# State-space scan of a decoder kernel: TensorE adds half of the decayed state, VectorE the other half by 256 columns

## The reference, cut to what matters

```
dA = exp(dt[..., None] * A)
h  = dA * h + dt[..., None] * B[:, None, :] * x[..., None]
y  = einsum('ben,bn->be', h, C)
```

## Time and profile before

| | |
|---|---|
| median of 3 runs | 6723.25 us (6720.93 to 6724.89) |
| span of the profiled execution | 6765.1 us |
| its granted TensorE clock, mean | 0.858 of full speed |
| busy in the span: PE, DVE, ACT, POOL | 73%, 77%, 50%, 47% |
| the stage of the change | about the first 2640 us |

### The profile page before, as it was taken

One profiled execution on the slowest core, in us unless ns is written; L12 is line 12 of the kernel. 1 busy time (PEld: TensorE's weight loads), 2 busy tenths in 40 slices (PEclk: granted clock), 3 DMA queues, 4 the chain that ended last, 5 costly groups with the idle time before them and its releaser, 6 DMA issues. The chain is left out here.

```text
span 6765.1 us, 148097 instructions
## 1 busy us (share of the span) xinstructions
PE 4948.8 (73%) x49380; PEld 2831.3 (42%) x49380; DVE 5218.7 (77%) x9423; ACT 3364.1 (50%) x4743; POOL 3159.4 (47%) x2904
## 2 busy tenths in 40 slices
PE   4777777777777776587775965899966647877890
PEld 1222222222222223365555543666645545666440
DVE  3999999999999997498886334677759947888344
ACT  3555555555655554355662210444446626777440
POOL 5433333333333422366652655555533317988443
PEclk8888888888888888699897986899978868999995
DMA  1111111111111112221112552000001112222343
GB/s 41 39 39 46 40 40 42 43 39 40 46 39 39 43 40 63 59 60 41 43 37 68 143 115 84 15 17 18 14 25 32 32 36 71 73 73 75 115 138 102
DMA packets 620376, 366.38 MB, mean 54 GB/s; under 512 B 67337, under 2 KB 601292, under 8 KB 619852
## 3 DMA queue, kind: packets, MB, share of 16 engines
q1 hardware_dynamic: 600524, 335.54, 17.8%
q0 software_dynamic: 11648, 21.26, 1.5%
q10 hardware_dynamic: 7680, 3.15, 0.2%
HBM read 204.83 MB, written 66.85 MB: 40 GB/s over the span
## 5 line engine op out<-in xcount | busy, mean ns | idle before, releaser
L1363 ACT ACTIVATE mb_dA<-ps,mb_a_neg 128x1024 f32<-128x1024 f32 x1008 | 1122.5, 1114 | 768.9 <-PE ps L1133 684.7
L1707 DVE TENSOR_TENSOR mb_m<-mb_dA,ps 128x512 f32<-128x512 f32 x2016 | 1284.6, 677 | 29.3 <-PE ps L1148 17.5
L1715 DVE TENSOR_TENSOR ps<-mb_m,ps 128x512 f32<-128x512 f32 x1984 | 1272.8, 685 | 42.3 <-PE ps L1148 42.1
L1148 PE MATMUL ps<-mb_ur,mb_bl 64*128 64x256 bf16 x4032 | 452.6, 308 | 495.3 <-DVE mb_m L1707 487.8
L1160 PE MATMUL ps<-mb_m,mb_cz 128*32 128x256 f32 x8064 | 745.5, 446 | 3.7 <-DVE mb_m L1707 2.6
L1148 PEld LDWEIGHTS ps<-mb_ur,mb_bl 64*128 64x128 bf16 x4032 | 122.3, 98 | 1044.5 <-DVE mb_m L1707 982.6
L1133 PE MATMUL ps<-mb_ur,mb_sel 64*128 64x256 bf16 x4032 | 455.3, 310 | 121.9 <-ACT mb_dA L1363 96.0
L677 POOL TENSOR_TENSOR x_p<-x_p,x_rec 128x2048 f32<-128x2048 f32 x64 | 231.7, 3620 | 212.2 <-DVE x_rec L838 212.1
L1133 PEld LDWEIGHTS ps<-mb_ur,mb_sel 64*128 64x128 bf16 x4032 | 154.6, 103 | 418.1 <-ACT mb_dA L1363 265.8
L1160 PEld LDWEIGHTS ps<-mb_m,mb_cz 128*32 128x32 f32 x8064 | 169.2, 115 | 269.9 <-issue 226.7
L1614 POOL TENSOR_TENSOR mb_ys<-mb_ys,mb_cbu 128x256 f32<-128x256 f32 x64 | 46.6, 728 | 487.3 <-ACT mb_ys L1444 487.3
(11 more groups left out here) (494 smaller groups left out, 13041.2 us busy)
## 6 DMA issues: line engine op xcount, KB each, us to landing
mb_ur<-mb_pc SPq DMA_DIRECT2D x768, 64.0 KB
mb_bl<-mb_pc SPq DMA_DIRECT2D x576, 64.0 KB
ef_w<-in_ef_w SPq DMA_DIRECT2D x35, 514.5 KB
mx_w<-in_mx_w SPq DMA_DIRECT2D x39, 384.0 KB
moe_made<-mx_y SPq DMA_DIRECT2D x39, 256.0 KB
ea_wqk<-in_ea_wqk SPq DMA_DIRECT2D x70, 129.0 KB
ea_wvo<-in_ea_wvo SPq DMA_DIRECT2D x70, 128.5 KB
ea_x<-hidden SPq DMA_DIRECT2D x280, 32.0 KB, 2.0
```

Of the source, the lines that this page charges most:

```text
L1148: mm = nc.tensor.matmul(ps[:, UB + 2 * (t % 2) + g, 256 * pl:256 * pl + 256], bl[k, j % 2, tl, 128 * pl:128 * pl + 128], ur[k, j % 2, tl], ...
L1363: nc.scalar.activation(dA[:, t % RING].rearrange("p (g n) -> p g n", g=2), ps[:, DT:DT + 2, :], ACT.Exp, scale=a_neg[:, 0:1]).then_inc(dA_ ...
L1707: nc.vector.tensor_tensor(m[:, t % RING, half], dA[:, t % RING, half], ps[:, UB + 2 * ((t - 1) % 2) + g, :], ALU.mult).then_inc(m_ready.se ...
L1715: nc.vector.tensor_tensor(u, m[:, t % RING, 512 * g:512 * g + 512], u, ALU.add).then_inc(h_ready.sem, 1)
```

## The change

The bank `g = 1` of the state (`PE_PART`, columns 512 to 1023) is no longer added by DVE. DVE multiplies it by its decay (`decay_pe_part`, 512 columns), and PE adds `m` onto the outer product that already stands in the bank, as a product with the identity (`add_decayed`, `start=False`). The other bank stays with DVE, in two parts of 256 columns each (`decay_part`, `add_part`). The next `decay_pe_part` waits for the product of PE (`hp_ready`).

```diff
+        PE_PART = slice(512, 1024)
+        DVE_PARTS = [slice(0, 256), slice(256, 512)]
...
                 def outer(i, t):
...
-                                                  start=True, stop=True)
+                                                  start=g == 0 or pl == 0, stop=g == 0, skip_group_check=g == 1)
                     mm.then_inc(ub_done.sem, 1)
+
+                def add_decayed(i, t):
+                    pe.wait_ge(mp_ready.sem, mp_ready.at(i, t))
+                    nc.tensor.matmul(state(t, PE_PART), ident[:], m[:, t % RING, PE_PART], start=False, stop=True,
+                                     skip_group_check=True).then_inc(hp_ready.sem, 1)
...
                     for t in range(T):
...
+                        if 1 <= t < T - 1:
+                            add_decayed(i, t)
                         if t + 3 < T:
                             spread_dt(i, t + 3)
...
-                def decayed(i, t, g):
...
-                def advanced(i, t, g):
...
+                def decay_pe_part(i, t):
+                    dve.wait_ge(dA_ready.sem, dA_ready.at(i, t))
+                    dve.wait_ge(y_summed.sem, before(y_summed, i, t))
+                    if t == 1:
+                        dve.wait_ge(ub_done.sem, ub_done.at(i, 1))
+                    else:
+                        dve.wait_ge(hp_ready.sem, hp_ready.at(i, t - 1))
+                    nc.vector.tensor_tensor(m[:, t % RING, PE_PART], dA[:, t % RING, PE_PART], state(t - 1, PE_PART),
+                                            ALU.mult).then_inc(mp_ready.sem, 1)
...
                     for t in range(T):
                         j, tl = t // 16, t % 16
                         if t >= 1:
-                            decayed(i, t, 0)
-                            decayed(i, t, 1)
+                            decay_pe_part(i, t)
+                        if t >= 2:
+                            add_part(i, t - 1, 0)
+                            add_part(i, t - 1, 1)
...
-                        if 1 <= t < T - 1:
-                            advanced(i, t, 0)
-                            advanced(i, t, 1)
+                        if t >= 1:
+                            decay_part(i, t, 0)
+                            decay_part(i, t, 1)
```

More of the change, by code:

```diff
@@ L1007, in mamba @@
         ub_done = st.counter("ub_done", T - 1)
-        m_ready = st.counter("m_ready", 2 * (T - 1))
-        h_ready = st.counter("h_ready", 2 * (T - 2))
+        mp_ready = st.counter("mp_ready", T - 1)
+        md_ready = st.counter("md_ready", 2 * (T - 1))
+        hp_ready = st.counter("hp_ready", T - 2)
+        hd_ready = st.counter("hd_ready", 2 * (T - 2))
         y_summed = st.counter("y_summed", T - 1)
@@ L1018, in mamba, with state @@
         y_ready = st.counter("y_ready")
+        PE_PART = slice(512, 1024)
+        DVE_PARTS = [slice(0, 256), slice(256, 512)]
+        def state(t, cols):
+            g = cols.start // 512
+            return ps[:, UB + 2 * (t % 2) + g, cols.start - 512 * g:cols.stop - 512 * g]
         def xc(u, f, j):
@@ L1139, in outer @@
                     if t >= 2:
-                        pe.wait_ge(m_ready.sem, m_ready.at(i, 2 * (t - 1)))
+                        pe.wait_ge(md_ready.sem, md_ready.at(i, 2 * (t - 1)))
                     else:
-                        pe.wait_ge(m_ready.sem, m_ready.at(i - 1, 2 * (T - 1 - t)))
+                        pe.wait_ge(md_ready.sem, md_ready.at(i - 1, 2 * (T - 1 - t)))
                     if tl == 0:
@@ L1157, in contract @@
                         pe.wait_ge(y_taken.sem, y_taken.at(4 * i + j - 1))
-                    pe.wait_ge(m_ready.sem, m_ready.at(i, 2 * t))
+                    pe.wait_ge(mp_ready.sem, mp_ready.at(i, t))
+                    pe.wait_ge(md_ready.sem, md_ready.at(i, 2 * t))
                     for pr in range(4):
@@ L1361, in decay @@
                     act.wait_ge(dt_done.sem, dt_done.at(i, t))
-                    act.wait_ge(m_ready.sem, before(m_ready, i, t, 2))
+                    act.wait_ge(md_ready.sem, before(md_ready, i, t, 2))
                     nc.scalar.activation(dA[:, t % RING].rearrange("p (g n) -> p g n", g=2), ps[:, DT:DT + 2, :], ACT.Exp, scale=a_neg[:, 0:1]).then_inc(
@@ L1696, in weigh_bc @@
                     nc.vector.tensor_reduce(cb[:], cb_prod[:], AX.X, ALU.add).then_inc(cb_ready.sem, 1)
-                def decayed(i, t, g):
[L1699 to L1703, removed]
-                    if t > 1:
[L1705 to L1708, removed]
@@ L1711, in advanced, with decay_part, add_part @@
+                def decay_part(i, t, g):
+                    if t > 1:
+                        dve.wait_ge(hd_ready.sem, hd_ready.at(i, 2 * (t - 2) + g + 1))
+                    cols = DVE_PARTS[g]
+                    nc.vector.tensor_tensor(m[:, t % RING, cols], dA[:, t % RING, cols], state(t - 1, cols),
+                                            ALU.mult).then_inc(md_ready.sem, 1)
+                def add_part(i, t, g):
                     if g == 0:
                         dve.wait_ge(ub_done.sem, ub_done.at(i, t + 1))
-                    dve.wait_ge(m_ready.sem, m_ready.at(i, 2 * (t - 1) + g + 1))
@@ L1714, in advanced @@
-                    u = ps[:, UB + 2 * (t % 2) + g, :]
-                    nc.vector.tensor_tensor(u, m[:, t % RING, 512 * g:512 * g + 512], u, ALU.add).then_inc(h_ready.sem, 1)
+                    dve.wait_ge(md_ready.sem, md_ready.at(i, 2 * (t - 1) + g + 1))
+                    cols = DVE_PARTS[g]
+                    h = state(t, cols)
+                    nc.vector.tensor_tensor(h, m[:, t % RING, cols], h, ALU.add).then_inc(hd_ready.sem, 1)
                 def output(i, j):
```

## The result

The changed kernel takes **6933.1 us** (median of 4 runs, 6929.96 to 6937.52) against 6723.18 (6720.93 to 6724.89) for the kernel before on the same chip: a ratio of 1.0313, 95% interval 1.0301 to 1.0326, or +210 us. The forecast was 7035 with 6935 to 7165.

What follows compares the result with a forecast made beforehand. DVE was taken to bound the kernel before, PE after the change: 169.4 us of PE work + 4.3 stalls + 3.5 clock = 177.2 us a chunk against 157.7, +312 us over 16 chunks, giving 7035 us, range 6935 to 7165.

Steps and rivals of the forecast that it cites:

- PE's work alone is longer than the chunk of today: Main point: PE's products in a chunk, start to start at full clock, sum to 169.4 us against 157.7.
- The ring: DVE multiply, hand-over to PE, add, hand-over back: 1.91 us, under PE's 2.27 us step, so priced at nothing.
- the low clock stays: Rival, chance 0.08: PE keeps 28% of its time at the lower clock level, 7363 us.
- the slow handshake: Rival, chance 0.05: slower DVE-PE hand-overs cost 0.2 us in some 37 plain steps a chunk, 7153 us.
- The add is cheaper: Rival, chance 0.05: hidden weight loads make each of 62 adds cost 0.86 us, 6837 us.
- 62 adds x 1.06", "14 extras x 1.06", "17 small extras x 0.64: PE's work in a chunk: add_decayed 65.7 us, other products of 512 columns 14.8, small ones such as gates 10.9.
- 19.5 us: Growth forecast for each of 16 chunks, from 157.7 to 177.2 us, giving +312 us.
- Idle PE: Stalls of PE a chunk: 2.1 us behind norm and 2.2 behind silus, together 4.3 us.
- the 0.36 of slack: Plain step: the 1.91 us from DVE's multiply through PE's add back to DVE is 0.36 under PE's 2.27.
- The clock: Lower PE clock only behind the norm and silus stalls: 3.5 us a chunk, from 0 to 6.
- faster: Rival, chance 0.04: DVE stays the bound, an add costing 0.53 us as one record, 6504 us.
- the break-even: Price of each of 62 adds at which a chunk takes as long as before: 0.75 us.

Runs made afterwards that it cites:

- a mix by steps: Kernel before, with TensorE adding only in steps without an extra product, TensorE's products reordered, norm's two small operations on GpSimd: 6587.6 us, ratio 0.9785.
- the same order and `norm` and the add in all steps: Changed kernel with TensorE's order spread_dt, extra product, add_decayed, contract, outer, and norm's two small operations on GpSimd: 6796.7 us, ratio 1.0100.

## Why the prediction was right or wrong

**Right in kind.** "PE's work alone is longer than the chunk of today" holds: doubling a group on PE costs all of its 0.22 us a step after the change and nothing before it, the plain step is 2.27 us to the hundredth, and DVE waits in it. The ring is not the bound: PE waits for the multiply 50 us in the whole kernel. The rise of the clock to 0.98 came as forecast, so "the low clock stays" is out, and with the plain step at 2.27 so is the slow handshake. None of the four rivals happened. "The add is cheaper" was the nearest, but it gave its 0.2 us to every add, and the plain step shows that it isn't there.

**Wrong in size, +312 forecast and +210 measured.** From its first multiply to its last, the stage ran from 112.86 to 2624.8 us before and runs from 113.03 to 2837.8 now, 212.8 us longer. (The two spans differ by 170.5 only, because what stands behind the stage was 42 us longer in the profiled execution of the kernel before.) Two terms of the sum account for it.

1. *The extras' and adds' prices were start-to-start distances with another neighbour.* Rows 5 give 1.06 ahead of bf16 work, and rows 6 give 0.64 ahead of bf16 work. In the changed kernel nearly each extra stands ahead of the add, and the pair costs 0.2 us less; the prediction turned this saving down by rows 5, which have no such pair. The 33 pairs make 6.6 us; with `turn_y` (0.28 measured, 0.44 charged) PE's work in a chunk is about 162.3 us, not 169.4. The step that failed is the list "62 adds x 1.06", "14 extras x 1.06", "17 small extras x 0.64".
2. *19.5 us were charged to 16 chunks.* The last two chunks have fewer extras. By the windows shown first they take 158.58 + 146.77 = 305.4 us; the kernel before took 154.67 + 152.23 = 306.9 for them, by these windows of it:

```profile
2320.10:2474.77 154.67, 112.54 (x1082) 40.14 (x1082) 151.12 (x259) 89.71 (x102) 54.17 (x39) 0.82 0.15 40
2474.77:2627.00 152.23, 101.94 (x1044) 36.95 (x1040) 150.70 (x256) 76.08 (x83) 16.26 (x18) 0.81 0.11 29
```

The 39 us charged to them are not there. The sum holds for 14 chunks, which grew by (212.8 + 1.6) / 14 = 15.3 us each, from 157.7 to 173.0.

Against these stand the stalls, which were charged too little. With each start-to-start distance on PE set against the same distance at full clock, the first 14 chunks of the trace take 162.3 us of work, 6.8 of idle PE and 3.9 of lower clock on average, together 173.0; 169.4, 4.3 and 3.5 were forecast.

- *Idle PE, 6.8 for 4.3.* `norm` stops PE for 3.5 us a chunk, and 2.1 was forecast, because GpSimd now holds DVE for 2.26 us in one instruction instead of about 1: `norm` keeps DVE from 1393.59 to 1397.66, 4.07 us for 2.47, and less the 0.36 of slack that is 3.7. `silus` stops PE for 2.6 (2.2 forecast). The rest is 0.2 in nearly every chunk and 1.5 to 3.2 us at the boundary behind three of them.
- *The clock, 3.9 for 3.5.* This term was right. The lower level comes behind `norm` in each of the 14 chunks, by these windows of one:

```profile
1398.00:1402.00 4.00, 3.61 (x19) 1.22 (x20) 3.58 (x10) 1.61 (x3) 3.92 (x2) 0.73 0.02 4
1402.00:1406.00 4.00, 4.00 (x28) 0.90 (x30) 2.46 (x7) 1.11 (x1) 2.25 (x2) 0.84 0.00 0
```

Behind `silus` it comes in some chunks and not in others, after the same 2.54 us of idle PE. In one, `contract` ran at the lower level (1.01 us from start to start, a record of 1.08) and the add behind it took 2.01; in another, `contract` ran at full clock (a record of 0.64):

```profile
997.58 0.61 PE L1142 MATMUL ps<-mb_ur,mb_sel 64*128 64x256 bf16 x4 [2.54 <-ACT mb_dA L1380]
998.11 1.08 PE L1175 MATMUL ps<-mb_m,mb_cz 128*32 128x256 f32 x8
999.12 0.61 PE L1157 MATMUL ps<-mb_ur,mb_bl 64*128 64x256 bf16 x4
999.66 2.08 PE L1164 MATMUL ps<-mb_m,mb_ident 128*128 128x512 f32 x2
1001.67 0.61 PE L1142 MATMUL ps<-mb_ur,mb_sel 64*128 64x256 bf16 x4
...
1343.36 0.39 PE L1142 MATMUL ps<-mb_ur,mb_sel 64*128 64x256 bf16 x4 [2.54 <-ACT mb_dA L1380]
1343.68 0.64 PE L1175 MATMUL ps<-mb_m,mb_cz 128*32 128x256 f32 x8
```

The balance: (-7.1 + 2.5 + 0.4) x 14 = -59, and -39 - 1.5 for the last two chunks, from +312, is +212. So the forecast came as near as it did partly because two errors, work too dear and stalls too cheap, have opposite signs.

**What stays open.** Why GpSimd's instruction comes upon `norm` as it does in 14 of 16 chunks of the changed kernel is only argued: GpSimd's work is released by ACT and PE, and shifted with them against DVE. In the kernel before GpSimd was at work beside `norm` in these 14 chunks too, but one of the two small instructions was held there for 0.8 to 1.0 us and the other for nothing. What decides whether the clock falls behind `silus` was not tested. And "faster" by a mix was not forecast at all: the break-even was set for the add in every step, and a mix by steps, which is what wins, was not among the cases.

## What to carry to other kernels

Moving work from the engine that is full to one that "waits" pays only up to the point where both take the same time in the same step. So it is read from start-to-start distances with the extras counted, and given only to the steps that have room (0.9785 against 1.0100 with the same order and `norm` and the add in all steps; the two also differ in DVE's pieces, 512 against 256 columns, which gave nothing where PE was full). The price of a short TensorE instruction belongs to its neighbours: take it from a row with the same instruction ahead of it and behind it, and group f32 products with full weights, and bf16 groups, next to each other. Count the repetitions for which the sum holds; the last rounds of a pipeline have less work beside them.

## What the runs showed of the hardware that was not expected

- An f32 product with 128x128 weights right behind another such product: the pair takes 1.92 us for 512 columns, against 2.12 apart. Ahead of `contract` (128x32 weights), and in a plain step ahead of bf16 groups, it stays at 1.06. The Trainium skill ("TensorE: Matmul & The Clock Gate", "Step-by-step: what each phase is for") has the next weights loaded while the present product runs. The traces show it only between neighbours of one kind: behind an extra the add's load starts 0.11 us ahead of the product (1304.55 and 1304.66 in the changed kernel), in a plain step both start at 1301.84. That this load makes up the whole 0.2 us is not shown.
- A bf16 group of four takes 0.23 us ahead of another bf16 group and 0.32 ahead of an f32 product.
- VectorE's addition of 128x4 numbers, both inputs in SBUF, took 0.16 us with GpSimd idle and 2.26 us in 14 of 16 times in the changed kernel, when it met a GpSimd `tensor_tensor` of 1024 columns, and ended with it. VectorE's instructions that read PSUM beside GpSimd kept their 0.69. Taking the two small operations off VectorE gave 61 us in the changed kernel and 15 in the kernel before. The Trainium skill ("SBUF — State Buffer", "Terms") describes a port pair that the two engines lock for a whole instruction. The trace agrees for these `tensor_tensor`, but not beside a GpSimd `tensor_scalar` in the kernel before, where the addition started just behind it and ended 2.6 us ahead of its end (GpSimd from 333.74 for 3.63 us, the addition from 333.77 for 1.02).
- With a second `spread_dt` in each step of the kernel before, the granted clock of one stretch was 0.96 instead of 0.86, and the time stayed the same.
